# First one-hots of each node group in buffers of their own, and groups spread over more feature products

## The reference, cut to what matters

```python
edge_index = jnp.stack([src, dst])                    # dst is sorted, and dense at low node numbers
xn = _layernorm(x, axis=-1)
x1 = jax.nn.relu(xn @ W_ah + b_ah)                    # the "feature products"
loops = jnp.arange(N); src, dst = concat(edges, loops)
e = leaky_relu(as_n[src] + ad_n[dst], 0.2)            # in each attention layer
m = segment_max(e, dst); p = exp(e - m[dst]); s = segment_sum(p, dst)
out = segment_sum(p / s[dst] * h[src], dst)
```

## Time and profile before

| | us |
|---|---|
| median of 3 runs (range) | 1384.36 (1382.99 to 1387.48) |
| the profiled execution, its own time | 1384.69 |
| its span, first to last instruction | 1382.8 |
| PE busy in the span | 1305.9 (94%) |
| DVE busy in the span | 993.8 (72%) |
| ACT busy in the span | 509.9 (37%) |
| mean granted TensorE clock | 0.989 of full speed |

### The profile page before, as it was taken

How to read it: one execution, slowest core, us unless ns; L and a number is a source line. 1 busy time by engine, 2 the same in 40 slices (tenths; PEclk the granted TensorE clock), 3 DMA queues, 4 the chain that set the end, 5 groups by cost and what they waited for, 6 DMA issues and landing times.

```text
span 1382.8 us, 20288 instructions
## 1 busy us (share of the span) xinstructions
PE 1305.9 (94%) x7907; PEld 1222.0 (88%) x7907; DVE 993.8 (72%) x1724; ACT 509.9 (37%) x844; POOL 44.4 (3%) x52
## 2 busy tenths in 40 slices
PE   5998889999997998999999999999999999999886
PEld 5655538999997998999999999999999999999785
DVE  7546596999998525867675776677666766778667
ACT  5333323334444404434323432433243334323373
POOL 5000000000000230000000000000000000000000
PEclk9999999999999999999999999999999999999998
DMA  9110002122212938100101200120111011105003
GB/s 256 71 69 1 35 2 90 54 90 92 91 57 63 273 106 237 72 1 38 41 1 72 70 8 34 39 78 1 72 38 41 1 72 38 43 1 146 0 1 112
DMA packets 23508, 90.11 MB, mean 65 GB/s; under 512 B 3537, under 2 KB 4878, under 8 KB 20347
## 3 DMA queue, kind: packets, MB, share of 16 engines
q1 hardware_dynamic: 22495, 86.57, 19.4%
q10 hardware_dynamic: 924, 2.30, 0.5%
HBM read 77.80 MB, written 11.06 MB: 64 GB/s over the span
## 4 chain that ended last, share of the span: by engine, by line
PE 54%; DVE 7%; ACT 1%; issue 1%; DVEq 0%
PE psum L1738 26%; PE psum L105 8%; PE psum L106 8%; PE psum L107 8%; DVE hN L1362 1%; PE psum L1752 1%; DVE prob L1346 1%; DVE prob L1340 1%; PE psum L1792 1%; DVE acc L1384 0%; DVE x1l L1369 0%; DVE acc L1400 0%; PE psum L1807 0%; ACT prob L1568 0%; DVE xll L1375 0%
## 5 line engine op out<-in xcount | busy, mean ns | idle before, releaser
L1738 PE MATMUL psum<-hN,prob 125*125 125x193 f32 x2400 | 409.0, 327 | 1.5 <-DVE hN L1362 1.5
L1738 PEld LDWEIGHTS psum<-hN,prob 125*125 125x125 f32 x2400 | 395.4, 187 | 2.0 <-issue 1.8
L1568 ACT ACTIVATE prob<-prob,acol 125x1250 f32<-125x1250 f32 x120 | 160.9, 1341 | 381.5 <-DVE prob L1340 381.5
L1346 DVE SCALAR_TENSOR_TENSOR prob<-prob,cnt 125x1250 f32<-125x1250 f32 x120 | 174.7, 1456 | 56.4 <-ACT prob L1568 56.4
L1340 DVE SCALAR_TENSOR_TENSOR prob<-vrow,ncol,urow 125x1250 f32<-125x1250 f32 x120 | 181.9, 1516 | 9.5 <-PE psum L1738 9.5
L781 DVE CUSTOM_DVE_ANT_0 junk<-mask,arow 125x1250 bf16<-125x1250 uint8 x120 | 174.8, 1457 | 3.1
L105 PE MATMUL psum<-woh,xlh 128*125 128x384 f32 x360 | 127.3, 354 | 2.6 <-DVE acc L1384 2.6
L106 PE MATMUL psum<-wol,xlh 128*125 128x384 f32 x360 | 122.6, 341 | 0.0
L105 PE MATMUL psum<-wph,x1h 128*125 128x384 f32 x330 | 117.8, 357 | 4.8 <-PEq L997 1.9
L107 PE MATMUL psum<-woh,xll 128*125 128x384 f32 x360 | 122.0, 339 | 0.0
L107 PE MATMUL psum<-wph,x1l 128*125 128x384 f32 x330 | 111.2, 337 | 0.0
(11 more groups left out here) (247 smaller groups left out, 2202.2 us busy)
## 6 DMA issues: line engine op xcount, KB each, us to landing
arow<-scratch_a SPq DMA_DIRECT2D x12, 625.0 KB, 4.0
urow<-scratch_uv SPq DMA_DIRECT2D x12, 625.0 KB, 4.1
vrow<-scratch_uv SPq DMA_DIRECT2D x12, 625.0 KB, 5.9
wT<-in_w_turned SPq DMA_DIRECT2D x6, 1152.0 KB, 8.1
wq_raw<-in_w_qkv SPq DMA_DIRECT2D x6, 1152.0 KB, 6.8
wp_raw<-in_w_pair SPq DMA_DIRECT2D x6, 1152.0 KB, 7.5
wo_raw<-in_w_out SPq DMA_DIRECT2D x6, 1152.0 KB, 5.1
xN<-in_x SPq DMA_DIRECT2D x10, 336.0 KB
```

The lines of the kernel that those rows point to most:

```text
L1346: nc.vector.scalar_tensor_tensor(prob[n % RING][:, :], prob[n % RING][:, :], 1.0, cnt[:, n % NT, :], op0=ALU.min, op1=ALU.mult).then_inc(p ...
L1568: nc.scalar.activation(prob[n % RING][:, :], prob[n % RING][:, :], ACT.Exp, bias=acol[:, n // NT, n % NT:n % NT + 1]).then_inc(e_ready, 1)
L1738: last = nc.tensor.matmul(bank(t // 2)[0:P, 193 * (t % 2):193 * (t % 2) + 193], ring[:, t * P:(t + 1) * P], hN[i % 2][:, j, 193 * s:193 * ...
```

## The change

Twelve more buffers hold the one-hots of the first four units of a group: four pairs and two parts for groups 0 to 7 in a part of x1T that is not yet written, and as many for groups 8 to 24 where weights lay that are no longer needed. DVE makes these four outside the loop, waiting for PE to have used the same four of the group before (`first_free`). PE uses them outside the loop (`first_ready`). The loops on both engines begin four units later and use the ring as before. The index arrays are padded to ET + 2 CE. The groups are dealt out by `BESIDE`: products 8 to 12 and 17 hold two each, 13 to 16 hold three (before k = 2, before k = 4 and after the product), and group 24, the densest, comes last of all, behind `turn_scores`. The lowest score is reduced between the first four units of group 24 and its loop, and ACT shifts the scores and rounds the weights ahead of taking group 24.

```diff
-        src_f, dst_f = at("src_f", Z + 1280, [P, ET + CE - 1]), at("dst_f", Z + 1952, [P, ET + CE - 1])
+        src_f, dst_f = at("src_f", Z + 1280, [P, ET + 2 * CE]), at("dst_f", Z + 1952, [P, ET + 2 * CE])
+        first_pair = [[at(f"first_pair{e}", whole(X1_AT + ROW * e + 3000), [P, WN], BF16) for e in range(CE)],
+                      [at(f"later_pair{e}", S + 1024 * e, [P, WN], BF16) for e in range(CE)]]
+        first_part = [[at(f"first_part{q}", whole(X1_AT + ROW * (CE + q) + 3000), [P, 2, 128], BF16) for q in range(CE // 2)],
+                      [at(f"later_part{q}", S + 1024 * CE + 512 * q, [P, 2, 128], BF16) for q in range(CE // 2)]]
...
-        FIRST, EARLY = 8, 20
+        BESIDE = {8 + j: {3: 2 * j, KT: 2 * j + 1} for j in range(5)}
+        BESIDE.update({13 + j: {2: 10 + 3 * j, 4: 11 + 3 * j, KT: 12 + 3 * j} for j in range(4)})
+        BESIDE[17] = {3: 22, KT: 23}
+        TAKEN = 8
...
-        SCORED, HAS = 7, (1, 0, 2, 1, 0)
-        LOW_AT, SHIFT_AT, WQ_AT = 21, 21, 22
+        SCORED, HAS = 9, (1, 0, 2, 1, 0)
+        LOW_AT = NW - 1
...
@@ vector: for n, w in enumerate(WINDOWS)
-                with dve.Fori(bounds[w][0], bounds[w][1], CE) as unit:
+                pairs, parts = first_pair[n >= TAKEN], first_part[n >= TAKEN]
+                for e in range(CE):
+                    if e % 2 == 0:
+                        if n:
+                            dve.wait_ge(first_free, CE * (n - 1) + e + 2)
+                        nc.vector.tensor_tensor(parts[e // 2][:, :, 0:P], place[:, 0:P].unsqueeze(1).to_broadcast([P, 2, P]),
+                                                part_h[:, bass.ds(bounds[w][0] + e, 2)].unsqueeze(2).to_broadcast([P, 2, P]), ALU.is_equal)
+                    nc.vector.tensor_scalar(pairs[e][:, :], place[:, :], float(WN * w), pair_f[:, bass.ds(bounds[w][0] + e, 1)],
+                                            ALU.add, ALU.is_equal).then_inc(first_ready, 1)
+                if n == LOW_AT:
+                    dve.wait_ge(at_ready, len(CH))
+                    own.done(nc.vector.tensor_reduce(low[:, :], abT[0:HEADS, :], axis=AX.X, op=ALU.min))
+                    nc.vector.tensor_scalar(minus_low[:, :], low[:, :], -1.0, None, ALU.mult).then_inc(a_low, 1)
+                with dve.Fori(bounds[w][0] + CE, bounds[w][1], CE) as unit:
...
@@ tensor: hidden(i), for k in range(KT)
-                    if i >= FIRST and k == KT // 2:
-                        window(2 * (i - FIRST))
...
+                    if k in BESIDE.get(i, {}):
+                        window(BESIDE[i][k])
...
@@ tensor: window(n)
-                with pe.Fori(bounds[w][0], bounds[w][1], CE):
+                pairs, parts = first_pair[n >= TAKEN], first_part[n >= TAKEN]
+                for e in range(CE):
+                    pe.wait_ge(first_ready, CE * n + e + 1)
+                    nc.tensor.matmul(here, parts[e // 2][:, e % 2, 0:P], pairs[e][:, :], start=False, stop=False,
+                                     skip_group_check=True).then_inc(first_free, 1)
+                with pe.Fori(bounds[w][0] + CE, bounds[w][1], CE):
...
             turn_scores()
-            for n in range(EARLY, NW):
-                window(n)
-                if n in MASKED_AT:
-                    turn_mask(MASKED_AT[n])
+            window(NW - 1)
```

## The result

| | before | changed |
|---|---|---|
| median, first comparison | 1385.80 us (4 runs) | 1371.15 us (4 runs, 1368.83 to 1372.79) |
| ratio, first comparison | | 0.9887, 95% interval 0.9865 to 0.9909 |
| ratio, repeated (`changed_again`) | | 0.9888, interval 0.9858 to 0.9917 |
| the profiled execution, its own time | 1384.69 us | 1372.78 us |
| opening of group 0 | 56.5 us | 59.3 us |

The kernel is 1.1% faster, some 15.6 us. The stretch that the change touches got 16.9 us shorter in this profile. The whole execution got 11.9 us shorter (11.8 by its span), because 2.8 us were lost ahead of the groups and 2.3 us behind them. Whether these two belong to the change is one question of the experiments.

The account below looks back on a forecast made before the run. DVE bounds groups 20 to 24, PE elsewhere, each waiting through a ring of four. Losses removed less new work open group 23 at 170.5; plus 22.5 closes group 24 at 193.0, 17.0 us earlier: 1367.5 us, range 1363.5 to 1375.

Parts of the forecast that it names:

- Depth: Fifteen groups of eight units beside products: DVE finishes eight units before PE opens the group, so 17.2 us of loss go whole.
- Extra rounds: Five groups of at most four units: the loop runs at least once, 20 more units, 4.2 us on PE.
- Group 0: First group: its eight units can't be ready, because DVE starts at 55.77; it loses 1.2 us.
- Groups 20 to 22: Each has four units beyond the eight, which come late: a loss of 1.1 us each, 3.3 in all.
- The opening of group 23: PE begins the units of group 23 at 170.5 us instead of 187.88.
- The end: Groups 23 and 24: DVE sets the time, 22.5 us against 22.1 now, so they gain nothing; `turn_scores` and mask 8 hide.
- The sum: Group 24 closes at 193.0 us instead of 209.96, 17.0 us earlier, and all that follows shifts with it.
- the clock: Dip of the granted clock from 213 to 217 us, behind the groups: may fall otherwise, up to 2 us either way.
- (a): Rival: first pairs 0.2 us slower, gaps in products 13 to 16 lose; 7 us of gain gone, 1374.5 us; chance 0.18.
- (b): Rival: group 0 and groups 20 to 22 lose nothing and extra rounds hide; below 1364 us, 1363 at lowest; chance 0.06.
- (c): Rival: 12 taken back edges in groups 20 to 24 must be fetched; 1386.5 to 1395 us; chance 0.05 together with (d).
- (d): Rival: first four units come no earlier, only the new order remains, extra units cost 4.2 us; 1387; chance 0.05 with (c).

Follow-up runs that it names:

- bufs_only: Changed kernel with the groups and the lowest score in the old order, only the buffers kept; stretch 139.2 us, ratio to before 0.9890.
- order_only: Changed kernel without the blocks for the first four units, so new order with the old ring of four; stretch 155.6 us, ratio to before 0.9997.
- no_extra: Changed kernel with the loop skipped in groups 0, 1, 3, 4 and 8; stretch 134.1 us, ratio to before 0.9860.
- scores_first: Changed kernel with `turn_scores` ahead of mask 8 and SCORED set to 8; stretch 136.1 and 136.3 us, ratio to before 0.9869.
- The dose: Changed kernel with a small write and a wait added to each pair of first units; stretch 139.7 us.
- deep_end: The kernel with `turn_scores` before mask 8, plus 8 first units for groups 20 to 22, 12 for 23, 16 for 24; stretch 128.0 us, ratio 0.9825.
- all_in: `deep_end` and `no_extra` together; stretch 122.9 us, total 1354.98 us, ratio to before 0.9754.
- the third profile: Third of four profiles of the unaltered changed kernel; stretch 138.0 us.

## Why the prediction was right

**Depth.** Right. The 17.2 us of the fifteen groups of eight units went whole (group 14: 1.68 us, no wait), and `bufs_only` against `order_only` shows that they went through the buffers. **Extra rounds.** Right: 20 units more, and the loop runs at least once. `no_extra` gives 5.05 us back up to group 23. Group 0 took 62.18 - 59.53 = 2.65 us, a loss of 1.0 against the 1.2 forecast. **Groups 20 to 22** kept their third four late. Group 22 took 164.94 - 161.27 = 3.67 us instead of 12 x 0.21 = 2.52, a loss of 1.15 where 1.1 was forecast, and 20 and 21 the same. **The opening of group 23.** Its units were to begin at 170.5, counted from an opening of group 0 at 56.46, so after 114.0 us. They began after 172.61 - 59.31 = 113.3, 0.7 earlier. Group 0 accounts for 0.2 of it; where the rest lies was not followed up.

**The end.** Here a term was mis-sized, by 0.8 us. I forecast 22.5 us from the first unit of group 23 to the closing of 24 and it was 195.91 - 172.61 = 23.3. I had written that `turn_scores` and mask 8 hide behind DVE. They do not quite. `turn_scores` also waits for ACT to copy mask 8, since SCORED = 9 asks for 27 freed parts, and with that 1.8 us group 24 opens too late for the full ring (the pair at 182.06). Of the waits that SCORED = 9 brings, I had named that of mask 9 and not this one. `scores_first`, without this wait, came to 22.7.

**The sum.** 17.0 us forecast for the stretch, 16.9 in the profile. That it fits so closely is luck twice over. The opening of group 23 came 0.7 us too early for the forecast and the end took 0.8 too long, and the two cancel. And this was the one profile of four without the half clock: the other three gave 15.3 to 15.7. The forecast allowed 2 us either way for the clock, for the dip behind the last group; that one would come around the opening of group 24 was not foreseen. The total moved by 1.1%, 15.6 us by the ratio of both comparisons, where 17 were forecast. The 2.8 us ahead of the groups, which made the profiled execution look poorer, are part of the scatter of that opening (53.4 to 59.3 us).

**The rivals.** (a) The pace of first pairs did not fall (178.42 to 179.26 is one pair in 0.84 us). The dose showed that its price was put too high, since PE's gaps with a mask take most of it up. (b) did not happen as the change was written. Its 1364 us are passed only with more depth at the end (`deep_end` 1361.92, `all_in` 1354.98); taking the extra rounds out alone gives 1367.92. (c) The 37 branches on DVE took 43 to 78 ns, none more, and the 37 on PE 76 to 231 ns (57 of 76 to 225 before). The Trainium skill ("Runtime: NRT & Kernel Launch", Instruction fetch mechanics) warns of taken branches that leave the pages held; no branch of either kernel shows such a stop. (d) did not happen: groups 1 to 19 came with all eight units ready. `order_only`, at a ratio of 1.000, is what it would have been without the extra units.

## What to carry to other kernels

Where two engines each wait for the other through a small ring and both have idle time, suspect the depth of the ring first. Here it was the loss. Count how many items the faster side takes in one go and how many the slower one can make in the gap, and compare these with the number of slots. Here, dealing the same work out in another order gained nothing without the slots, and at most 1.0 to 2.6 us with them. When a step is moved behind others, list all that its semaphore count asks for, the copies by a third engine too.

## What the runs showed of the hardware

The granted clock fell to one half in PE's thinly used stretch between groups 23 and 24 in three of four executions of the same kernel, and stayed at 1.00 in the other. The rows of the third profile show 0.97 and 0.59 in the windows around it. As a duration: in that profile the first four units of group 24 stand 0.42 us apart (176.82 to 178.48) and at full clock 0.21 (182.07 to 182.91 in the profile after). Where DVE feeds PE at 0.85 us a pair, a pair fits even at half clock. So the fall cost time only where PE had ready units to take.

The first group opened anywhere between 53.4 and 59.3 us in executions of one kernel. A single profile's total therefore can't tell a gain of a few us, while the stretch between two events of the same block repeated to 0.1 us up to group 24.
